# The four sixteen-head attention stages: DRAM stack laid out piece by piece, norms of batches 2 to 7 placed between other work

## The reference

```
x = x + L0_attn_b(layernorm(x))    # stage l0b: no causal mask, heads regrouped through DRAM ("grouped")
x = x + L2_attn_a(layernorm(x))    # stage l2a: rotary positions, causal
x = x + L2_attn_b(layernorm(x))    # stage l2b: causal, output norm
x = x + L3_attn_a(layernorm(x))    # stage l3a: rotary positions, causal
# each: q, k, v = layernorm(x) @ W;  e = exp(scale * q k^T - rowmax);  out = (e v) / sum(e) [@ Wo + bo]
```

## Time and profile before

| | us |
|---|---|
| median of 3 runs | 4628.32 (4628.16 to 4641.85) |
| the profiled execution | 4627.72, span 4626.0 |
| l0b, first statistics to first scoresT | 514.5 to 604.3 |
| l2a, the same | 2189.6 to 2267.2 |
| l2b, the same | 2871.5 to 2944.6 |
| l3a, the same | 3527.7 to 3606.1 |

### The profile page before, as it was taken

How to read it: one execution, slowest core, us unless ns; L and a number is a source line. 1 busy time by engine, 2 the same in 40 slices (tenths; PEclk the granted TensorE clock), 3 DMA queues, 4 the chain that set the end, 5 groups by cost and what they waited for, 6 DMA issues and landing times. The chain is left out here.

```text
span 4626.0 us, 67869 instructions
## 1 busy us (share of the span) xinstructions
PE 3021.5 (65%) x23727; PEld 1870.4 (40%) x23727; DVE 2815.2 (61%) x5972; ACT 1710.7 (37%) x3042; POOL 2095.7 (45%) x2616
## 2 busy tenths in 40 slices
PE   5758267765294549667677745677565787566856
PEld 3658011111294238456233334333243333244534
DVE  4634476674445963432676578577586766496768
ACT  2413156564131224433355412455422445323511
POOL 6552320100343532232345376254594444496676
PEclk9879578897597769878699867799776899676867
DMA  5022222220131012011222000322001222000000
GB/s 153 38 76 69 64 77 67 58 52 1 60 95 47 0 53 63 14 39 53 69 72 64 22 1 0 84 65 76 2 1 28 71 70 57 1 0 1 1 0 19
DMA packets 218177, 206.37 MB, mean 45 GB/s; under 512 B 50439, under 2 KB 195015, under 8 KB 217080
## 3 DMA queue, kind: packets, MB, share of 16 engines
q1 hardware_dynamic: 205560, 176.85, 13.8%
q0 software_dynamic: 12288, 25.19, 1.8%
HBM read 103.55 MB, written 96.47 MB: 43 GB/s over the span
## 5 line engine op out<-in xcount | busy, mean ns | idle before, releaser
L923 DVE TENSOR_REDUCE l0b_negm<-l0b_ps_s 128x2 f32<-128x1024 f32 x256 | 304.5, 1220 | 146.6 <-PE l0b_ps_s L699 145.8
L787 ACT ACTIVATE l0b_E<-l0b_ps_t 128x1024 f32<-128x1024 f32 x256 | 262.0, 1023 | 201.5 <-PE l0b_ps_t L681 201.1
L923 DVE TENSOR_REDUCE l3a_negm<-l3a_ps_s 128x2 f32<-128x256 f32 (+3 forms) x256 | 198.9, 818 | 93.8 <-PE l3a_ps_s L705 93.4
L923 DVE TENSOR_REDUCE l2b_negm<-l2b_ps_s 128x2 f32<-128x256 f32 (+3 forms) x256 | 199.0, 818 | 88.2 <-PE l2b_ps_s L705 87.6
L923 DVE TENSOR_REDUCE l2a_negm<-l2a_ps_s 128x2 f32<-128x256 f32 (+3 forms) x256 | 198.8, 818 | 87.0 <-PE l2a_ps_s L705 86.7
L787 ACT ACTIVATE l3a_E<-l3a_ps_t 128x768 f32<-128x768 f32 (+1 forms) x192 | 169.2, 881 | 186.9 <-PE l3a_ps_t L681 186.7
L787 ACT ACTIVATE l2a_E<-l2a_ps_t 128x768 f32<-128x768 f32 (+1 forms) x192 | 169.4, 882 | 184.2 <-PE l2a_ps_t L681 183.9
L787 ACT ACTIVATE l2b_E<-l2b_ps_t 128x768 f32<-128x768 f32 (+1 forms) x192 | 169.4, 882 | 151.2 <-PE l2b_ps_t L681 151.1
L867 POOL TENSOR_SCALAR_AFFINE_SELECT l3a_E<-l3a_E 128x256 f32<-128x256 f32 x256 | 101.4, 409 | 221.1 <-ACT l3a_E L787 218.9
L867 POOL TENSOR_SCALAR_AFFINE_SELECT l2a_E<-l2a_E 128x256 f32<-128x256 f32 x256 | 101.4, 409 | 219.2 <-ACT l2a_E L787 216.9
L867 POOL TENSOR_SCALAR_AFFINE_SELECT l2b_E<-l2b_E 128x256 f32<-128x256 f32 x256 | 101.3, 410 | 219.1 <-ACT l2b_E L787 218.9
(11 more groups left out here) (1003 smaller groups left out, 9501.2 us busy)
## 6 DMA issues: line engine op xcount, KB each, us to landing
l0b_stack<-l0b_q_piece SPq DMA_DIRECT2D x48, 128.0 KB
l0b_stack<-l0b_k_piece SPq DMA_DIRECT2D x48, 128.0 KB
room_up<-l0b_stack SPq DMA_DIRECT2D x32, 192.0 KB, 3.4
room_down<-l0b_stack SPq DMA_DIRECT2D x32, 192.0 KB, 4.3
l2a_stack<-l2a_q_piece SPq DMA_DIRECT2D x48, 128.0 KB
l2a_stack<-l2a_k_piece SPq DMA_DIRECT2D x48, 128.0 KB
room_up<-l2a_stack SPq DMA_DIRECT2D x32, 192.0 KB, 4.1
room_down<-l2a_stack SPq DMA_DIRECT2D x32, 192.0 KB, 5.0
```

The source lines that it names most:

```text
L787: act.activation(probs(n % 3, c, 0)[:, 2 * p:2 * p + 2, :], ps_t[:, :, 0:width[c]], ACT.Exp, scale=scale).then_inc(probs_ready.sem, 1)
L923: e = dve.tensor_reduce(negm[:, qt, :, j], ps_s[n % 2][:, :, off:off + keys[qt]], AX.X, ALU.max, negate=True)
```

## The change

The stack in DRAM becomes [2, 6 blocks, 4 groups, 8, 4, 512]: one block is 128 rows of 1 KB in one run. A piece is stored to all of its blocks by one DMA whose source is repeated, so q takes three DMAs and k three, with the same bytes. The load of a half takes the same 48 rows of 4 KB, which now lie in six runs of 8.

The loops change too. The norm of batch 1 is done ahead of the loops, wholly. For batches 2 to 7, four tables give the index of each step of the norm: `counted` (statistics), `rooted`, `shifted` and `normed` (normalise, transposes and their reading). POOL splits q of batch 0 in one go at index 2 (5 in l0b), and the ones go out at index 0.

```diff
-Q_ROWS = ((0, 8, 24), (16, 40), (32,))
-K_ROWS = ((0, 16, 32), (8, 40), (24,))
+Q_ROWS = (slice(0, 3), slice(4, 6), slice(3, 4))
+K_ROWS = (slice(2, 5), slice(0, 6, 5), slice(1, 2))
-        stack = nc.dram_tensor(f"{name}_stack", [2, 4, STACK, 4, S], BF16).ap()
+        stack = nc.dram_tensor(f"{name}_stack", [2, BLOCKS, 4, HD, 4, S], BF16).ap()
-        def normed_at(T):
-
-            n = (T + 2 * STEPS - L) // 2 + 1
-            return n if T >= L - 2 * STEPS and T % 2 == 0 and n < B else None
+        def named(table, T):
+
+            return [n for n, at in table.items() if at == T + 2 * STEPS]
+
+        counted = {n: n - 2 for n in range(2, B)} if grouped else {2: 0, 3: 1, 4: 2, 5: 7, 6: 8, 7: 9}
+        rooted = {n: n - 1 for n in range(2, B)} if grouped else {2: 1, 3: 3, 4: 4, 5: 8, 6: 9, 7: 10}
+        shifted = {n: n for n in range(2, B)} if grouped else {2: 1, 3: 7, 4: 8, 5: 9, 6: 10, 7: 11}
+        normed = {n: L + 2 * n for n in range(2, B)} if grouped else {2: 5, 3: 9, 4: 25, 5: 27, 6: 29, 7: 31}
+        split_at = 5 if grouped else 2
@@ store_pieces
-                for part, rows in zip(piece[a], (Q_ROWS, K_ROWS)[a]):
-                    for r in rows:
-                        sp.dma_start(stack[a, :, r:r + HD].rearrange("b r c s -> b (r c) s"), part[:, :]).then_inc(pieces_stored[a].sem, 16)
+                for part, places in zip(piece[a], (Q_ROWS, K_ROWS)[a]):
+                    copies = len(range(*places.indices(BLOCKS)))
+                    sp.dma_start(stack[a, places].rearrange("k b d c s -> (b d c) k s"),
+                                 part[:, :].rearrange("p (a s) -> p a s", a=1).broadcast_to([P, copies, S])).then_inc(pieces_stored[a].sem, 16)
@@ place_stack
-                                     stack[a, 2 * hh + half]).then_inc(stack_ready[half].sem, 16)
+                                     stack[a, :, 2 * hh + half].rearrange("k d c s -> k d (c s)")).then_inc(stack_ready[half].sem, 16)
@@ sync
-                if T == -L:
+                if T == -2 * STEPS:
@@ tensor
             rows.transposes(pe, 0)
+            rows.transposes(pe, 1)
             for T, b, g, l in steps():
-                if normed_at(T) is not None:
-                    rows.transposes(pe, normed_at(T))
+                for n in named(normed, T):
+                    rows.transposes(pe, n)
@@ scalar
-            rows.normalise(act, 0)
-            rows.read_transposes(act, 0)
+            for n in range(2):
+                rows.normalise(act, n)
+                rows.read_transposes(act, n)
@@ gpsimd
-                if normed_at(T) is not None and normed_at(T) >= 2:
-                    rows.roots(pool, normed_at(T))
+                for n in named(rooted, T):
+                    rows.roots(pool, n)
+                if T == split_at - 2 * STEPS:
+                    for k in range(6):
+                        split(pool, ch, 0, 0, k)
@@ vector
             rows.statistics(dve, ch, 1)
+            rows.shifts(dve, 1)
-                if normed_at(T) is not None:
-                    rows.shifts(dve, normed_at(T))
-                    if normed_at(T) + 1 < B:
-                        rows.statistics(dve, ch, normed_at(T) + 1)
+                for n in named(shifted, T):
+                    rows.shifts(dve, n)
+                for n in named(counted, T):
+                    rows.statistics(dve, ch, n)
```

More of the change, by code:

```diff
@@ L463, in heads_attention_stage @@
     VROW = H * VW + 32 - VW
-    projected, normed = wo is not None, out_norm is not None
-    PLACES = sum(len(rows) for rows in Q_ROWS)
+    projected, out_normed = wo is not None, out_norm is not None
+    PLACES = len(Q_ROWS)
+    BLOCKS = STACK // HD
     with ExitStack() as ctx:
@@ L493, in heads_attention_stage @@
         y = sb("y", [P, TB, D])
-        if normed:
+        if out_normed:
             stats = sb("stats", [P, TB, 6])
@@ L815, in read_grouped_values @@
                     a.then_inc(spare_read.sem, 1)
-            rows.normalise(act, 0)
-            rows.read_transposes(act, 0)
+            for n in range(2):
+                rows.normalise(act, n)
+                rows.read_transposes(act, n)
             for T, b, g, l in steps():
-                if normed_at(T) is not None:
-                    rows.normalise(act, normed_at(T))
-                    rows.read_transposes(act, normed_at(T))
+                for n in named(normed, T):
+                    rows.normalise(act, n)
+                    rows.read_transposes(act, n)
                 if T == -STEPS:
@@ L882, in finish_output @@
                 x = (core.XN if grouped else core.X)[:, n * TB:(n + 1) * TB, :]
-                if normed or grouped:
+                if out_normed or grouped:
                     pool.wait_ge(out_ready.sem, out_ready.upto(n + 1))
@@ L897, in _ @@
                 k = T % STEPS - 5
-                if 0 <= k < 12 and 0 <= b + 2 < B and not (b + 2 == 0 and k >= 6):
+                if 0 <= k < 12 and 1 <= b + 2 < B:
                     split(pool, ch, b + 2, k // 6, k % 6)
-                if g == 2 and l == 3 and normed and 0 <= b - 1 < B:
+                if g == 2 and l == 3 and out_normed and 0 <= b - 1 < B:
                     pool.wait_ge(stats_ready.sem, stats_ready.upto(b))
                     pool.tensor_tensor(rstd[:, :], var[:, :], core.minus_half[:, 0:TB], ALU.pow).then_inc(rstd_ready.sem, 1)
-                if g == 3 and l == 0 and normed and 0 <= b < B:
+                if g == 3 and l == 0 and out_normed and 0 <= b < B:
                     add_bias(b)
@@ L996, in add_output @@
                     dve.wait_ge(out_read.sem, out_read.upto(n))
-                if not normed:
+                if not out_normed:
                     dve.tensor_tensor(y[:, :, :], po, bo[:, :].rearrange("p (a d) -> p a d", a=1).broadcast_to([P, TB, D]),
@@ L1053, in _ @@
                     split_maxima(2 * (b + 1))
-                if g == 3 and l == 0 and normed and 0 <= b - 1 < B:
+                if g == 3 and l == 0 and out_normed and 0 <= b - 1 < B:
                     normalise(b - 1)
-            if normed:
+            if out_normed:
                 normalise(B - 1)
@@ L1066, in heads_attention_stage @@
     pv_ready.per, pv_read.per = B * QUADS * NC, B * QUADS
-    bias_added.per = B * normed
-    stats_ready.per = rstd_ready.per = B * normed
-    out_ready.per = B * (normed or grouped)
+    bias_added.per = B * out_normed
+    stats_ready.per = rstd_ready.per = B * out_normed
+    out_ready.per = B * (out_normed or grouped)
     out_read.per = B
```

## The result

The kernel after took 4513.5 us, the median of four executions (4508.6 to 4519.5), the kernel before 4631.3 beside it: ratio 0.9742, 95% interval 0.9721 to 0.9763. On the 4628.3 of the forecast that is 4509 us, 119 us less (110 to 129), where the forecast had 87 less and a range that ended at 4512. A second pair on another chip gave 0.9741 (0.9714 to 0.9768). The direction and the places of the gain were right; the sum was a quarter too small.

What follows compares the result with a forecast made beforehand. Latency chains bound the four stage beginnings, PE the rest of l2a; 60.9 us off beginnings, 23 off later waits and 3 for clock make 87, so 4628 becomes 4541 us. Range 4525 to 4558, reaching into rivals 4512 to 4580.

Steps and rivals of the forecast that it cites:

- Two chains: Stage beginnings: stores and loads, and seven norms, end together at the first scores; shortening one alone would win little.
- Norms and splits: l2a's beginning: q ready at 2210.3, not 2217.6, k at 2213.9; PE's list reaches the first scores at 2230.8.
- Stores: Beginnings: six stores on 16 engines, not twelve on 4; the last lands at 2219.5, from a span of 2219.6 to 2225.
- Loads: Beginnings: six engines, not 16, carry each load; a half takes 8.0 to 12.4 us, there at 2230 in l2a.
- rival B: Loads on six engines at 13 GB/s or less hold up beginnings and later batches: costs 28 us, 4569; chance 0.17.
- D: Rival: loads still run when a batch's second mT is issued, stopping each batch: slower, 4707 us; chance 0.03.
- From scores to the first scoresT: Beginnings: 17.25 us to mT stays, plus 1.5; mT's flight shortens; first scoresT in l2a 14.3 us earlier.
- Later batches: Batch starts after each stage's first: PE's 25.3 us of waits for mT go, counted as 23.
- the discount: Later batches: only nine tenths of the 25.3 us counted, since ACT's and PE's own alternation is late next.
- the term for it: PE's clock after the beginnings: fewer stops may hold it up, worth 3 us.
- Rival A: PE's clock falls hang on the mT waits; a third of the low-clock time returns: 4519 us; chance 0.14.
- sign for A: PE's clock rising above 0.95 in l2a and l3a would show the clock rival.

Runs made afterwards that it cites:

- e1: Kernel before with only the new DRAM stack, its six stores and its loads; norms, split and ones as before: ratio 0.9861.
- e2: Kernel after with the stack, twelve stores and loads of before; norms, q's split and ones in their new places: ratio 0.9929.
- e4: Kernel after with pieces innermost in the stack's rows and twelve stores, so that stores and loads both get 16 engines: ratio 0.9757.
- f2: Kernel after, unchanged, traced a second time on another chip: ratio 0.9741 to the kernel before there.
- e10: Kernel after with norms of batches 5 to 7 behind the first scores in causal stages, and stores and loads both on 16 engines: ratio 0.9754.
- e9: Kernel after with only the norms of batches 5 to 7 moved behind the first scores in the three causal stages: ratio 0.9746.
- e5: Kernel after with each place stored by itself, twelve stores in place of six, without repeated source: ratio 0.9759.
- pair 1: First traces of the kernels before and after, unchanged, compared with each other: ratio 0.9742.
- pair 2: Second traces of the kernels before and after, unchanged, both on one other chip: ratio 0.9741.
- e3: Kernel after with twelve stores, but batches 2 to 7 use a second DRAM tensor whose store pattern begins with 4 again: ratio 0.9816.
- e7: Kernel after with extra matmuls that nobody reads on PE in the beginnings, to raise its clock: ratio 0.9766.

## Why the prediction was too cautious

**Two chains, both cut: right.** e1 and e2 show it from both sides, and the 19 us that the beginnings of neither have alone are what the prediction said of a change that shortened one of them.

**Norms and splits: right in time, wrong in length.** q's pieces came at +20.3 (forecast +20.7), k's at +23.8 (+24.3). PE's list to the first scores took until +36.6, not +41.2, 4.6 us less. I had laid it out with projections each 2.9 to 3.1 us apart, which is PE at 1.2 GHz; in the traces of after they are 1.97 apart, as PE reaches 2.4 GHz at the second of them. By l3a of e2 that is 2.3 of the 4.6, or 3.2 by the estimate given there. The rest, 1.4 to 2.3, is in the layout itself, which was too long even for 1.2 GHz: the third transposes end at +26.8 and not +27.3, and the first projection of batch 1 at +28.5 and not +29.4. The last norm did hold PE, for 1.45 of the 1.5 us, but DVE's maxima hid all but 0.5 of it.

**Stores: mechanism right, landing mis-sized.** From the first store of k to the load I had 5.6 us and it took 3.5: 1.5 for three issues and 2.1 for the rest. The first load went 2.5 us earlier than forecast. I had put issue, transfer and completion one behind the other, while the first transfers run under the later issues.

**Loads: right, and dearer in the forecast.** The Trainium skill's rule (DMA: Bandwidth & Descriptors, "Why a DMA increments its semaphore by 16 and not by 1") gives six engines, and the trace agrees with 0.36 of 16. A half takes 8.8 us (l0b, 543.76 to 552.58), near the low end of 8.0 to 12.4; I had taken 10.5. An engine moves 21 GB/s then (126/6), not the 13 at which it ran among sixteen. Together with the stores this put the first half in by +36.6, where I had +40.4. It had to be, for the earlier PE list to pay, but it adds nothing to it: the two chains run side by side. Of rival B's 28 us only some 3 to 4 came, by e4, nearly all in l0b, and of D nothing.

**From scores to the first scoresT: 2.6 us too long in l2a and l3a.** From the first scores to mT's issue it took 16.2 us, not 18.8, since part of it ran at 2.4 GHz. In l2a of f2, the same list with PE back at 1.2 GHz behind the first scores, it took 18.2, so 2.0 of the 2.6 us are the clock. In l2b, where the clock stayed at 0.53, it took 18.3, as forecast. From mT's issue to scoresT 3.4, as forecast, with no wait.

**So in the beginnings the step that failed is the clock, with a layout of PE's list that was too long besides.** The prediction read 0.50 to 0.54 in the earlier trace rows and kept it for the new list. The shortfall is 7.1 us in each of l2a and l3a. PE's level makes 4.3 to 5.2 of it, 2.3 to 3.2 ahead of the first scores and 2.0 behind them (e10 has 4.0), the layout 1.4 to 2.3, and half a us is the rest. It is 1.8 and 1.3 in l2b and l0b, where the clock hardly rose. At the low clock l2a of e9 has +61.3, near the +63.3 of the forecast.

**Later batches: right, and the discount was not needed.** All 25.3 us of waits went, not nine tenths. Nothing became late in their place. In the comparisons at like clock a rest gained 13 to 15 where 12 were in the waits and 11 counted. The clock came on top, and here too the term for it failed: I had put 3 us on it for all stages. A rest without waits is 5 us shorter at 0.955 and more than at 0.93. l2a had 0.970 in after, f2 and e5, though not in e4 (0.936), whose engines have the same lists; l3a had 0.956 and 0.932 in after and f2, from 0.927 and 0.922 before. In l0b's rest the clock went the other way (0.880 to 0.845 in pair 1, 0.854 to 0.839 in pair 2) and the rest got 6 and 8 us longer. Over all traces that rest spans 513.8 us at 0.873 to 527.0 at 0.839, and neither the layout nor the order goes with it: e2, with the old layout, has 526.8, e4 513.8, and e5, which differs from after in the stores alone, 515.7.

**Rival A came nearest in time (4519), by a mechanism that is half right.** It had PE's clock fall because of the waits. The falls at the batch starts do: 35 of 48 with the waits, none of 108 without, and e3 brings eight of twelve back by one edit. By the prediction's own sign for A, a clock above 0.95 in l2a and l3a, the first trace of after says yes (0.970, 0.956) and the second only in l2a. What A had wrong is that nothing would take their place. e1, e4 and e7 have no waits and still 0.925 to 0.938, with the long falls inside batches; and e2 and e3 have the waits and 0.955 and 0.959 in l2a. So the price of A's falls is small: e3's rests are longer than e5's by 1.4 us (l2a) and 5.2 us (l3a) more than the waits. The rest of the clock's part varies between executions. What sets off the long falls, and why the same list takes one level in l2a and another in l3a, is open.

**The range.** It reached 29 us below the forecast, 7 below rival A, and the time was 3 us further down. Three terms had been taken on the costly side of what their rows allowed (the landing of stores and loads, a tenth off the waits, the low clock), and a range around such a sum has to reach further down than up; mine did the reverse.

## What to carry over

Before a change to a start-up chain is priced, look which of its durations were taken at PE's low level, and give the sum once with them at each level: 4 us a stage came of that here, in l2a and l3a. When a clock is compared before and after, look where its falls stand and not only at its mean. Count the engines of a DMA from the first dimension on both sides, stores and loads apart: four engines for stores that everyone waits for cost 25 us of waits in later batches and, by e1, 24 in the four beginnings, while six for loads that are mostly hidden cost 3 to 4. When two chains end together, forecast and try them as one change, and put short work that others wait for in one go ahead of operations that wait for a third engine.

## What the hardware showed that I had not expected

One instruction list in one execution runs at either level of PE's clock: in e10 l2a's projections took 1.13 us and l3a's 2.08, in the same place. The Trainium skill (TensorE: Matmul & The Clock Gate, "Part 1: The HAM clock gate") states that one kernel's clock rises at another point from run to run; the trace agrees, and shows it between two stages of one run, with its price. A DMA engine is not a fixed number of GB/s: it moved 13 (210/16) or 12.5 (200/16, e4) with all sixteen on a load and 21 to 26 (126/6, 158/6 in another window of l2a's loads) with six, at a busy share near full in both, so that ten engines fewer cost 2.5 us of 8.8 for a half. In l2a and l3a PE fell to 1.2 GHz at 35 of the 48 batch starts at which it waited some 2 us for mT, and at none of the 108 without that wait. And issuing a load took SP 0.72 to 0.80 us with a pattern of six leading places and 0.4 with 48 rows, while a store of e4 to 16 engines took 0.63: there SP's issue, not the engines (share 0.57), seems to have been the limit.
